# 64 of 200 pair steps per chunk turned to row form, their products summed on ScalarE

## What is computed

```python
vi = x[:, i_idx, :]; vj = x[:, j_idx, :]     # x: 2048 x 40 x 64, 780 pairs (i < j)
viW = jnp.einsum('bpd,pde->bpe', vi, W)      # W: 780 x 64 x 64
out = jnp.einsum('bpe,bpe->bp', viW, vj)     # 2048 x 780
h = jnp.concatenate([out, dense_ctx], axis=1)
h = jnp.maximum(h @ W_top1 + b_top1, 0.0)    # 796 -> 512
h = jnp.maximum(h @ W_top2 + b_top2, 0.0)    # 512 -> 256
y = h @ W_top3                               # 256 -> 1
```

## Time and profile before

| | |
|---|---|
| median of 3 runs | 1378.1 us (1376.8 to 1378.47) |
| the profiled execution, its own time | 1377.84 us |
| its span in the profile | 1376.0 us |
| granted TensorE clock, mean | 0.994 |
| PE busy | 1305.7 us, 95% |
| DVE busy | 926.0 us, 67% |
| POOL busy | 605.2 us, 44% |
| ACT busy | 77.8 us, 6% |

### The profile page before, as it was taken

The page is one execution under the profiler, slowest core; times in us unless marked ns, Lnnn a source line. Parts: engine busy times, 40 slices in busy tenths (PEclk is TensorE's granted clock), DMA queues, the critical chain, the costliest instruction groups (busy, mean ns, idle before and its releaser), DMA issues.

```text
span 1376.0 us, 16855 instructions
## 1 busy us (share of the span) xinstructions
PE 1305.7 (95%) x7024; PEld 463.0 (34%) x7024; DVE 926.0 (67%) x803; ACT 77.8 (6%) x97; POOL 605.2 (44%) x647
## 2 busy tenths in 40 slices
PE   1389999999999999999999999999999999999998
PEld 0133333333333333333333333333333333333333
DVE  0257888888656567787765666788776566788860
ACT  0000000000000000000000000000000000000001
POOL 6766443266754355766655456667660000000000
PEclk9989999999999999999999999999999999999999
DMA  4122221222222222222222223223221111111001
GB/s 151 26 62 62 57 70 52 68 61 65 82 54 68 66 72 75 62 82 63 63 59 82 63 66 87 61 62 83 63 62 52 52 54 52 53 44 54 1 1 42
DMA packets 36180, 84.43 MB, mean 61 GB/s; under 512 B 12420, under 2 KB 12420, under 8 KB 36104
## 3 DMA queue, kind: packets, MB, share of 16 engines
q1 hardware_dynamic: 11520, 52.43, 11.4%
q0 software_dynamic: 20560, 21.34, 7.9%
q10 hardware_dynamic: 4024, 9.58, 2.3%
HBM read 83.30 MB, written 0.01 MB: 61 GB/s over the span
## 4 chain that ended last, share of the span: by engine, by line
PE 92%; POOL 4%; issue 2%; DMA 1%; ACT 0%; DVE 0%; DVEq 0%; POOLq 0%
PE u L497 52%; PE zacc L512 27%; PE tacc L552 7%; PE u L471 3%; POOL gathered L312 2%; POOL first_fields L312 2%; PE tacc L555 2%; PE u L552 1%; DMA index<-ids 1%; PE u L555 1%; DMA gathered<-tbl,index 1%; PE tacc L559 1%; ACT h L369 0%; DVE prod L429 0%; DVEq L204 0%
## 5 line engine op out<-in xcount | busy, mean ns | idle before, releaser
L429 DVE TENSOR_TENSOR prod<-u,emb 128x1024 f32<-128x1024 f32 x800 | 925.8, 1216 | 409.2 <-PE u L497 409.2
L497 PE MATMUL u<-emb,weights 64*128 64x512 f32 x3200 | 753.6, 608 | 1.2 <-ACT emb L338 1.2
L312 POOL DMA_INDIRECT gathered<-tbl,index x512 | 482.9, 943 | 361.2 <-DVE prod L429 221.0
L497 PEld LDWEIGHTS u<-emb,weights 64*128 64x128 f32 x3200 | 291.6, 187 | 433.0 <-DVE prod L429 210.7
L512 PE MATMUL zacc<-prod,band 128*32 128x512 f32 x3200 | 391.7, 598 | 1.6 <-DVE prod L429 1.6
L512 PEld LDWEIGHTS zacc<-prod,band 128*32 128x32 f32 x3200 | 85.2, 109 | 278.9 <-DVE prod L429 147.9
L312 POOL DMA_INDIRECT first_fields<-tbl,index x128 | 120.8, 944 | 63.4 <-issue 32.6
L552 PE MATMUL tacc<-z,w12s 128*128 128x512 f32 (+1 forms) x196 | 97.4, 618 | 4.7 <-ACT h L369 4.7
L338 ACT ACTIVATE emb<-u 128x1024 f32<-128x1024 f32 x40 | 40.9, 1024 | 593.9 <-PE u L471 593.9
L552 PEld LDWEIGHTS tacc<-z,w12s 128*128 128x128 f32 (+1 forms) x196 | 33.2, 189 | 69.1 <-issue 59.5
L471 PE MATMUL u<-ident,first_fields 128*128 128x128 f32 x64 | 11.0, 318 | 43.4 <-DMA first_fields<-tbl,index 43.4
(11 more groups left out here) (17 smaller groups left out, 17.8 us busy)
## 6 DMA issues: line engine op xcount, KB each, us to landing
weights<-w_pairs SPq DMA_DIRECT2D x80, 640.0 KB
gathered<-tbl,index POOLq DMA_INDIRECT x512, 2.4
w12s<-w_top ACTq DMA_DIRECT2D x16, 448.0 KB, 3.3
first_fields<-tbl,index POOLq DMA_INDIRECT x128, 2.4
w12s<-w_top ACTq DMA_DIRECT2D x8, 256.0 KB, 2.5
index<-ids POOLq DMA_DIRECT2D x1, 320.0 KB, 7.2
z<-dense ACTq DMA_DIRECT2D x4, 32.0 KB, 1.8
y<-ysb ACTq DMA_DIRECT2D x4, 2.0 KB
```

The lines of the kernel that those rows point to most:

```text
L312: pool.indirect_dma_start(out=to, out_offset=None, in_=tables[2 * t + e], in_offset=bass.IndirectOffsetOnAxis(ap=index[:, col:col + 1].bit ...
L429: nc.vector.tensor_tensor(prod[:, (c * len(COLUMNS) + m) % PRING, :, :], products, x, ALU.mult).then_inc(prod_ready, 1)
L497: last = nc.tensor.matmul(u[:, b, h, :], weights[half, w:w + P], x, start=True, stop=True)
```

## The change

The pairs of tiles 4 to 19 with fields 0 to 7 (tiles 0 to 3) get row form. A row step ("row", t, s) takes 128 samples: their part of `emb` of tile t is the stationary operand, the weights of 8 fields (512 columns, 4 units) move, so a buffer of `u` holds samples on the partitions, and 2 x 8 runs of 64 products along the free axis. 16 tiles times 4 groups of samples make 64 row steps, which stand for 64 column steps. 136 column steps stay.

DVE multiplies the buffer with `first_fields` (the gathered rows, not transposed) into `row_prod`, now a ring of 3. Row products don't go through `sum_step`. Instead `reduce_rows` moves from DVE to ACT, where each row step becomes 16 ACTIVATE instructions (Copy, 128x64, in place) with `accum_out`, each writing one column of `row_sums`. In ACT's order the 16 stand three steps (`REDUCE_LAG`) behind the row step. DVE waits before a row step until the reduction three rows back is done.

`make_steps` spreads the rows: one every 1.6 columns, which with whole columns gives the pattern row, column, column from step 8 to step 197, 64 rows at exactly 3 steps' distance. Tiles are needed earlier than before: the two tiles of transpose group 3 from step 12 (18 before), group 4 from 21 (32), group 5 from 36 (50), group 6 from 57 (72), group 7 from 84 (98), group 8 from 117 (128), group 9 from 156 (162). `issue_step` and the transposes' places follow from these.

At the end of a chunk `turn_rows` transposes `row_sums` with 8 PE transposes into one buffer of `u`, and `copy_turned` copies it (128x1024) to two blocks of `z`; `z` keeps 7 blocks. Batches of sums fall from 50 to 34 per chunk. The ring of weights becomes 7 slots of 5 units (41 loads per chunk, 20 before). `ysb` becomes a row of `h1`, and `h2` lies in blocks 2 and 3 of `z`.

```diff
-ROW_TILES = []
+ROW_TILES = list(range(FT, T))
+ROW_EVERY = 1.6
+ROW_RING = 3
+REDUCE_LAG = 3
-SLOT = 10
-WRING = 5
+SLOT = 5
+WRING = 7
@@ make_steps
+    rows = [("row", t, s) for t in ROW_TILES for s in range(SUB)]
+    for m in range(len(columns) + 1):
+        while rows and (m == len(columns) or
+                        m >= max(present[rows[0][1]], next_row)):
+            step = rows.pop(0)
+            next_row = max(m, next_row) + ROW_EVERY
...
+        if m < len(columns):
+            steps.append(columns[m])
@@ make_order
             if n in ROWS:
-                out.append(("reduce", c, n))
+                reduces.append((c * N + n + REDUCE_LAG, c, n))
+            while reduces and reduces[0][0] <= c * N + n:
+                _, at, r = reduces.pop(0)
+                out.append(("reduce", at, r))
@@ scalar
+            def reduce_rows(c, n):
+                act.wait_ge(prod_ready, c * N + n + 1)
...
+                for h in (0, 1):
+                    for f in range(FF):
+                        q = (2 * ROW_TILES.index(t) + h) * FF + f
+                        x = row_prod[:, slot, h, f * DIM:(f + 1) * DIM]
+                        last = nc.scalar.activation(x, x, ACT.Copy, accum_out=row_sums[:, s, q:q + 1])
+                last.then_inc(rows_reduced, 1)
@@ vector
-                    if r:
-                        dve.wait_ge(rows_reduced, r)
+                    if r >= ROW_RING:
+                        dve.wait_ge(rows_reduced, r - ROW_RING + 1)
...
-            def reduce_rows(c, n):
-                dve.wait_ge(prod_ready, c * N + n + 1)
...
-                nc.vector.tensor_reduce(row_sums[:, s, q:q + 2 * FF].rearrange("p (h f) -> p h f", h=2),
...
@@ tensor, turn_rows
-                for s in range(SUB):
-                    last = nc.tensor.transpose(u[:, b, 0, s * P:(s + 1) * P], row_sums[:, s, :], ident[:, :])
+                for g in range(ROW_BLOCKS):
+                    for s in range(SUB):
+                        last = nc.tensor.transpose(u[:, b, g, s * P:(s + 1) * P],
+                                                   row_sums[:, s, g * P:(g + 1) * P], ident[:, :])
```

More of the change, by code:

```diff
@@ L42, in make_steps @@
 def make_steps():
-    steps, units, n_units = [], [], 0
[L50 to L55, removed]
-            for s in range(SUB):
[L57 to L69, removed]
+    columns, present = [], {}
+    for t in range(T):
+        present[t] = len(columns)
+        columns += [("col", k, t) for k in range(FT if t in ROW_TILES else 0, t)]
+        if t % 2:
+            columns.append(("half", t - 1))
+    rows = [("row", t, s) for t in ROW_TILES for s in range(SUB)]
+    steps, units, n_units = [], [], 0
+    row_units = {}
+    next_row = 0
+    for m in range(len(columns) + 1):
[3 more added lines that the diff above has]
+            next_row = max(m, next_row) + ROW_EVERY
+            if step[1] not in row_units:
+                n_units += -n_units % (WRING * SLOT) if n_units % (WRING * SLOT) > WRING * SLOT - FT else 0
+                row_units[step[1]] = n_units
+                n_units += FT
+            steps.append(step)
+            units.append(row_units[step[1]])
+        if m < len(columns):
+            steps.append(columns[m])
             units.append(n_units)
             n_units += 1
+    n_units += -n_units % SLOT
     return steps, units, n_units
@@ L77 @@
 WSLOTS = N_UNITS // SLOT
-assert WSLOTS * SLOT == N_UNITS and WSLOTS % WRING == 0
+assert WSLOTS * SLOT == N_UNITS
 COLUMNS = [n for n, s in enumerate(STEPS) if s[0] != "row"]
@@ L84 @@
 GROUP_BATCHES = ZSTEPS // SUMB
[L85 to L86 removed]
+ROW_BLOCK = GROUPS
+ROW_BLOCKS = len(ROW_TILES) * 2 * FF // P
+ZG = GROUPS + ROW_BLOCKS
 LAST_BLOCK = GROUPS - 1
@@ L102, with w_load, w_before @@
              for x in range(WSLOTS)]
+def w_load(c, s):
+    return c * -(-(WSLOTS - s % WRING) // WRING) + s // WRING + 1
+def w_before(c, s):
+    return (c, s - WRING) if s >= WRING else (c - 1, max(x for x in range(WSLOTS) if x % WRING == s))
 def z_place(m, h):
@@ L178, in make_order @@
                             out.append(tops.pop(0))
+    for _, at, r in reduces:
+        out.append(("reduce", at, r))
+        if r == ROWS[-1]:
+            turns.append((0, at))
     for _, c in turns:
@@ L271, in _ @@
                     if c or s >= WRING:
-                        done = c * N + SLOT_DONE[s - WRING] if s >= WRING else (c - 1) * N + SLOT_DONE[s - WRING]
-                        sp.wait_ge(u_ready, done + 1)
+                        at, last = w_before(c, s)
+                        sp.wait_ge(u_ready, at * N + SLOT_DONE[last] + 1)
                     at = s % WRING * SLOT * P
@@ L289, in _ @@
                     if t < FT:
-                        if c >= 2 and ROWS and t == 0:
+                        if c >= 2 and t == 0:
                             pool.wait_ge(prod_ready, (c - 2) * N + ROWS[-1] + 1)
@@ L358, in copy_turned @@
                 free_z(c, ROW_BLOCK)
-                nc.scalar.activation(z_block(c, ROW_BLOCK), u[:, BUFFER[o], 0, :], ACT.Copy).then_inc(z_copied, 1)
+                nc.scalar.activation(z[:, ROW_BLOCK:ROW_BLOCK + ROW_BLOCKS, :], u[:, BUFFER[o], :, :], ACT.Copy
+                                     ).then_inc(z_copied, 1)
+            def reduce_rows(c, n):
+                act.wait_ge(prod_ready, c * N + n + 1)
+                if c and n == ROWS[0]:
+                    act.wait_ge(rows_turned, c)
+                _, t, s = STEPS[n]
+                slot = (c * len(ROWS) + ROWS.index(n)) % ROW_RING
+                for h in (0, 1):
[4 more added lines that the diff above has]
+                last.then_inc(rows_reduced, 1)
             def copy_top(c, item):
```

42 lines of the change are left out of this document (17 added, 25 removed).

## The result

| | before | changed |
|---|---|---|
| median, us | 1377.47 | 1342.65 (1342.26 to 1342.97) |
| ratio | 1 | 0.9746 (95% interval 0.9731 to 0.9762) |
| span in the profile | 1376.0 | 1340.7 |
| PE busy | 1305.7 | 1242.6 |
| ACT busy | 77.8 | 1056.3 |

The forecast was 1340 us. One thing must be known to read the experiments: the kernel before took 1376.8 us beside two of the twelve runs and 1501 to 1515 us beside the other ten, for a reason that was not found, so times of those ten compare only with the kernel before beside them, while distances between batches of sums in the last chunk, ahead of its turn, repeat to 0.01 us in all.

The account below looks back on a forecast made before the run. PE's own work, busy 95% of the span, was taken as the bound. 1376.0 - 60 - 5 + 4 + 3 = 1318, late copies +20: 1338, and +1.8: 1340 us. Forecast range 1305 to 1375 (chance 0.50), wider range 1283 to 1525.

Parts of the forecast that it names:

- The removed sums: On PE, 64 row steps per chunk need no sums: 29.7 us less per chunk, 119 us over four.
- The sign that the prediction named: In the profile after, PE's busy time should fall by some 115 us.
- The rings: Between PE and DVE, a group of six steps takes 7.72 us; some 8 of 31 groups with a transpose escape.
- The sums' wait: Before each batch of sums PE waits 0.42 us for DVE's fourth product of the six steps.
- The reduction's price: On ACT, each small accumulating ACTIVATE takes 223 ns start to start, between 53 and 393 ns.
- its formula: ACT's excess per group of six at T per reduction: 32T + 0.5 - 7.72 us.
- The late copies: Copies to `emb` queue behind ACT's reductions, about 1 us short for half of 40 transposes: 20 us.
- Other queues: POOL's gathers, 5.0 us per field against 4.9 us of steps, SP's loads and DVE's wait for reductions: nothing added.
- The same reckoning: At chunk 0's start PE waits for gathers, so chunk 0 gains 5 us, not 30.
- The tail: At the end PE is held about 2 us for the last reductions, then the turn takes 1 us: +3.
- Rival A: ACT becomes the bound, no gain from 256 ns per reduction on, 1521 us at 300 ns; chance 0.36.
- Rival C: Reductions come out at 245 to 260 ns, gain and loss cancel: 1376 to 1380 us; chance 0.04.

Follow-up runs that it names:

- the run with one reduction: Changed kernel with 15 of each 16 reductions on ACT left out: 1469.6, 1488.1, 1473.1 us beside 1501.4, 1515.1, 1507.3 of the kernel before.
- the gathers' edit: Changed kernel with the gathers of late chunk 0 and of chunk 1 let go earlier: 1609.0 us beside 1515.1, 1577.1 beside 1507.3 of the kernel before.

## Why the prediction came right, and where it did not

**The removed sums (-119 us).** Right in size: PE's busy time fell by 63 us only because waits inside a group are counted as busy, but groups, steps and counts are as reckoned. The sign that the prediction named, a fall of some 115 us, was misjudged for that reason.

**The rings, and how few groups escape.** The new spacing's 7.72 us per group was measured as 7.70. The sums' wait was only half of the reason: the buffers of `u` bind 0.07 us behind. And transposes don't absorb the wait, as I had it for 8 groups of 31: most groups with a transpose and no top are 8.65 to 8.77 us, 7.70 and one transpose more, not the 7.30 + 1.02 = 8.32 of one that escapes. That is up to 8 x 0.42 = 3.4 us per chunk; chunk 2 gained 16.7 us where the prediction's terms give 18.7.

**The reduction's price.** Taken 223 ns, measured 239. The choice of the nearest row plus overlap was sound in result; what it consists of was not foreseen. The prediction names 241 ns as the price from which an excess shows, but its formula, 32T + 0.5 - 7.72, is positive from 226 ns on; 241 leaves the 0.5 out. The excess that 239 ns should have brought by the formula (0.43 us in 55 groups, 24 us) did not come. The reason is argued, not shown: the 0.5 us of ACT's other work does not lie in every group. A copy to `emb` comes only with a transpose, in a group that is a microsecond longer anyway, and the ring of 3 with a lag of 3 steps lets ACT run behind until then.

**The late copies, +20 us: wrong.** The waits are 4.3 us in all, 1.2 of them in the kernel before too. What filled their place is the start of chunk 1, 14 to 16 us. The step that failed stands under "Other queues": "a field's 5.0 us against 3.8 steps at 7.72 / 6 = 1.29, 4.9 us; nine steps are allowed for landing, so I take nothing". That compared rates and overlooked the need: fields 8 to 19 of chunk 1 are now asked for by step 21 of the chunk, not 32, while their releases, from step 182 to 204, are 2 steps apart and not 3.8; from 334 to 392 us POOL issues one gather each 1.25 us without a pause. The list of needed steps under "The change" showed it. The same reckoning was made for chunk 0 and gave 5 us of gain there; measured to the first pair step of chunk 1 it is 5.0 (352.6 after 357.6), and 3.5 in the table, which has the turn in it.

**The tail, +3 us.** It was 2 us of waiting and 1 us for the turn. The wait is 4.8 us, 4.5 of them ACT's by the run with one reduction, and the turn takes 1.9 at the lower clock. The prediction left out that the last row product itself ends only when PE's two steps behind the row are done as well, at 1293.4 us in the trace; ACT is then 0.9 us behind, and 16 reductions follow.

**So the number was right by luck, by errors that cancel.** Without the copies the prediction's terms give a gain of 58 us; 35.3 were measured. Of the 22.7 us between them 15.8 are missing in chunk 1, 4.8 in chunk 3 and the tail, 2.0 in chunk 2 and 0.2 before. The 20 us put down to copies covered them, while the copies' waits are about 3 us more than before. Rival A was not what happened, but its threshold is close: 0.239 us against the 0.256 at which I put the end of the gain, and 19 instead of 16 small reductions per row step already pace DVE. Rival C, 245 to 260 ns, was missed by 6 ns in its condition and by more than 30 us in time.

**What stays open.** Why the kernel before took over 1500 us beside ten of the runs. In their traces the extra time lies where gathers run, and single instructions last as long as otherwise (a product on DVE 1.21 us, a gather on POOL 0.95): it is time between instructions. There the kernels with all reductions took 1.028 to 1.086 of the kernel before, those with one sixteenth 0.974 to 0.983. So the gain of 2.5% is shown only beside a kernel before of 1377 us, and it may turn into a loss elsewhere: the changed kernel itself was not run there. Nor was the gathers' edit alone measured beside 1377 us. A fourth buffer of `u`, which would open the second ring, wasn't tried.

## To carry to other kernels

When a change takes work from the bounding engine, follow the nearest engine step by step through the ring of buffers before counting the gain: here a group of six could have gone from 8.24 us (1.5 x 5.49) to 7.21, and 0.49 of these 1.03 us went to waits between two engines that were 95% and 67% busy on average. A total that comes out right proves little before its terms are compared one by one, by chunk. Reckon what every queue must deliver by when, not only how fast it can: a schedule that asks for data 11 steps earlier needs its gathers let go earlier. Many small accumulating activations cost nothing where their engine has the room, at two overlapping instructions each; here the room was 7.65 of 7.70 us, and the copies that stand among them cost a few us in all, since the ring lets ACT run behind.

## Hardware behaviour that the runs showed

- An ACTIVATE of 128x64 with accumulator output from SBUF to SBUF is two records, 244 and 191 ns long. The reading starts 146 ns after the ACTIVATE and the next ACTIVATE 93 ns after the reading, on average: 239 ns for both. Of the two figures of the Trainium skill weighed in the prediction (VectorE: DVE Perf Modes, "The TRN2 errata"; ScalarE: Activation LUTs, "What ACT_TABLE_LOAD costs"), the duration of 240 ns agrees with the record's 244, and the overlapped distance of 146 ns with the 146 between ACTIVATE and reading; the reading, for which neither has a price, makes it 239. That an accumulator output makes two instructions, which the VectorE page says of VectorE, is so for ACT in this trace.
- On PE a change between pair matmuls (64x128) and sums (128x32) costs about 0.1 us ahead of the sums, 0.1 behind them and 0.14 within them, 0.33 us per batch (pair steps of 0.95 and 0.96 instead of 0.86 us; two batches of eight records per six steps 7.54 us, one of sixteen 7.21).
- At two waits of PE of 4.4 and 6.9 us the granted clock fell to the 1.2 GHz level (mean 0.79 from 372 to 380 us), and two pair steps took 3.48 us instead of 1.88. At the last turn's wait of 4.8 us it fell as well, and eight transposes took 1.88 us instead of 1.02.
